# Expert phase: gathers issued ahead of adds on GpSimd, up to three adds in flight within an expert, an expert's weights loaded in four transfers

## The chip, the cores and the metric

The kernel runs on one core of a Trainium2 chip. The metric is the device time of one execution in microseconds (us). The kernel before takes 837.55 us, the median of three runs (837.42 to 838.53).

## What is computed

The kernel is one layer of a network: gated cross-attention, then a gated mixture of experts. What is counted below is mostly the second part. Cut to what matters, the reference is:

```python
x = x + tanh(g_xattn) * cross_attention(layernorm(x), ctx)     # 8 batches x 256 rows x 512 columns, 16 heads
t = layernorm(x).reshape(2048, 512)                            # 2048 tokens
probs = softmax(t @ gate_w.T)                                  # 12 experts
top_w, top_i = top_k(probs, 2);  top_w = top_w / top_w.sum()
for e in range(12):                                            # w1, w3: 320 x 512, w2: 512 x 320
    h = silu(t @ w1[e].T) * (t @ w3[e].T)
    out = out + h @ w2[e].T * cw[:, e:e + 1]                   # cw: top_w of the token where e is picked, else 0
x = x + tanh(g_ffn) * out
```

Each token has two experts, so there are 4096 pairs of token and expert, which the kernel sorts by expert.

## The kernel before

The kernel has an attention phase over eight batches and an expert phase. All matrices of the expert phase are kept as two float16 parts (a high and a low one), and each product is three matmuls. While attention runs, ScalarE (ACT) loads each expert's weights in quarters, VectorE (DVE) splits them, and ACT stores them to `w_dram` (the profile says `weight_parts`), 2 MB per expert.

**Between the phases.** SP stores the last batch's sum to `out` (L469) and its normed tokens to `xn_dram` (L474, `tokens_normed`). SP and DVE wait for that store, then the engines read a flag and branch past a second, guarded attention run (`both_runs`, L291 to L294). ACT loads the weights of experts 0 and 1 into SBUF (`W`, L670 to L676), SP those of experts 2 to 11 (L490 to L504); `W` has room for four experts (`EB`), so expert e's load waits until the last tile of expert e-4 is done, and for the load before it. Each load is one transfer of 16 KB in each of 128 partitions. DVE sorts the pairs into 43 tiles of 128 (`TILES`; a tile holds one expert's tokens, and the last tiles may be empty) and makes `slot_tok`, `slot_out`, `slot_w` (which token, which row of `out`, which weight) and `table` (which expert, as the value that the weights' semaphore must have).

**The expert phase, per tile j.** GpSimd (POOL) gathers the tile's 128 token rows to `xg[j % 4]` with an indirect DMA (L579). TensorE (PE) turns them (`turn_x`, L1274, to PSUM), DVE copies them to `xT`. PE makes both hidden products (`hidden`, L1286); ACT and DVE make silu and the product and its two parts; PE turns these (`turn_h`, L1297), DVE copies them; PE makes the down product (`down`, L1307); ACT weighs it to `yo[j % 4]` (`weigh`, L703); POOL adds it to the rows of `out` with an accumulating indirect DMA (L593). The order on PE is written out in `step` (L1312 to L1326): in step j it reads `table` twice into registers (L1279), waits for the weights, and then runs `turn_h(j-1)`, `hidden(j)`, `turn_x(j+1)`, `down(j-1)`. `tiles` (L371) peels three steps, loops over rounds of four, and peels the rest.

**The order on POOL** is the loop at L588: wait for `yo` of tile j, wait until every earlier add has landed, issue add j, then issue gather j+4 (which reuses the buffer of tile j). The adds go one after another because an accumulating DMA reads and rewrites rows of `out`, and a token of one expert may come again in another expert's tile. Within one expert no token comes twice. On ACT, `weigh` waits until add j-4 has landed, so that `yo` is free.

Of the kernel before, what the change touches and what calls it, by code (L numbers as in the profile page):

```python
# [5 lines left out]
ALU = mybir.AluOpType  # L6
# [6 lines left out]
U16 = mybir.dt.uint16  # L13

P = 128
# [19 lines left out]
def wait(eng, sem, at, k, c=0, alone=None):  # L35

    if at.i is None and k * at.add + c <= 0:  # L40
        return
    assert k * at.add + c > 0, "a wait against nothing in a loop's first round"
    value = at.value(k, c)
    if alone is not None and at.i is not None:
        value = eng.to_reg(value)
        eng.wait_ge(alone, 1)
    eng.wait_ge(sem, value)
# [45 lines left out]
def flamingo_kernel(nc, x, ctx_in, g_xattn, g_ffn, WqT, bq, WkT, bk, WvT, bv, WoT, bo, gateT, wall, out):  # L93
# [3 lines left out]
    NE = gateT.shape[1]  # L97
    WCOL = wall.shape[2]
# [7 lines left out]
    TILES = (TOP * TOK + NE * (P - 1)) // P  # L106
# [9 lines left out]
    HOT = TOP * NT // 4  # L116
    LO = 2048.0
    TR = 4
    EB = 4
    HB = 2 * (FT - 1) + 1  # L120
    assert 2 * FL == P
# [16 lines left out]
    with top:  # L138
        def sb(name, shape, dt=F32, stack=top):
            return stack.enter_context(nc.sbuf_tensor(name, shape, dt))  # L140

        def sem(name):
            return top.enter_context(nc.semaphore(name))
# [109 lines left out]
        le = sb("le", [P, TILES, NE])  # L253
        et_f = sb("et_f", [P, TILES])
        table = sb("table", [P, TILES + NE], U16)
        xg = [sb(f"xg{i}", [P, 2 * T], F16) for i in range(TR)]
        xT = [sb(f"xT{i}", [P, 2 * TT, P], F16) for i in range(2)]
        act1 = [sb(f"act1_{i}", [P, F]) for i in range(2)]
# [93 lines left out]
        s_table = sem("s_table")  # L352
# [28 lines left out]
                step(eng, At(None, 0, n), n)  # L381


        s_add = sem("s_add")
        s_stored = sem("s_stored")
        s_spare = sem("s_spare")

# [6 lines left out]
        def _(sp):  # L394
# [95 lines left out]
            for e in range(EB // 2, NE):  # L490
                if e == EB:
                    sp.wait_ge(s_table, 2)
                if e >= EB:

                    end = sp.value_load(table[0:1, TILES + e - EB:TILES + e - EB + 1], min_val=1,
                                        max_val=TILES + 1)
                    sp.wait_ge(s_y, end)
                if e == NE - 1:
                    for n in range(2):
                        sp.wait_ge(s_wst[n], 16 * 2 * NE)  # L500

                sp.wait_ge(s_wr, 16 * e)
                sp.dma_start(W[:, (e % EB) * 2 * WCOL:(e % EB + 1) * 2 * WCOL],
                             w_dram[e].rearrange("p h n -> p (h n)")).then_inc(s_wr, 16)  # L504
            sp.wait_ge(s_wr, 16 * NE)


        @block.gpsimd
        def _(pool):
# [61 lines left out]
                    .then_inc(s_tilw, 1)  # L571


            pool.wait_ge(s_tok, 1)
            def gather(j):
                if j >= TR:
# [3 lines left out]
                                        in_offset=bass.IndirectOffsetOnAxis(ap=slot_tok[:, j:j + 1], axis=0))\  # L580
                    .then_inc(s_xg[j % TR], 16)

            for j in range(TR):
                gather(j)
            pool.wait_ge(s_tok, 2)
            pool.wait_ge(s_spare, 16 * TT)
            pool.wait_ge(s_stored, 1)
            for j in range(TILES):  # L588
                pool.wait_ge(s_yo, j + 1)
                if j >= 1:  # L590

                    pool.wait_ge(s_add, 16 * j)
                pool.indirect_dma_start(out=out[:, :],  # L593
                                        out_offset=bass.IndirectOffsetOnAxis(ap=slot_out[:, j:j + 1], axis=0),
                                        in_=yo[j % TR][:, :], in_offset=None, compute_op=ALU.add)\
                    .then_inc(s_add, 16)
                if j + TR < TILES:
                    gather(j + TR)
            pool.wait_ge(s_add, 16 * TILES)


        @block.scalar
        def _(act):
# [66 lines left out]
            for e in range(EB // 2):  # L670

                if e >= 1:

                    act.wait_ge(s_wr, 16 * e)
                act.dma_start(W[:, e * 2 * WCOL:(e + 1) * 2 * WCOL], w_dram[e].rearrange("p h n -> p (h n)"))\
                    .then_inc(s_wr, 16)  # L676

            act.wait_ge(s_wexp, 1)
            act.activation(el[:, :], dl[:, :], ACT.Exp).then_inc(s_wexp, 1)
# [17 lines left out]
            def weigh(act, j, n):  # L697

                wait(act, s_y, j, 1, 2)
                if n >= TR:  # L700

                    wait(act, s_add, j, 16, 16 - 16 * TR)
                act.activation(yo[n % TR][:, :], y_ps[:, :], ACT.Copy, scale=slot_w[:, bass.ds(j.value(), 1)])\  # L703
                    .then_inc(s_yo, 1)

# [15 lines left out]
        def _(dve):  # L721
# [16 lines left out]
            def done(ins):  # L738
                steps[0] += 1
                ins.then_inc(s_r, 1)  # L740
                return steps[0]
# [284 lines left out]
            for n in range(0, PAIRS, HOT):  # L1026
# [13 lines left out]
            then(last)  # L1040
            last = done(dve.tensor_reduce(et_f[:, :], le[:, :, :], AX_X, ALU.add))
            then(last)
            last = done(dve.tensor_scalar(et_f[:, :], et_f[:, :], float(NE - 1), None, ALU.min))
            then(last)
            dve.tensor_scalar(table[:, TILES:TILES + NE], endt[:, :], 1.0, None, ALU.add).then_inc(s_table, 1)
            dve.tensor_scalar(table[:, 0:TILES], et_f[:, :], 1.0, 16.0, ALU.add, ALU.mult).then_inc(s_table, 1)

            dve.wait_ge(s_tab, 2)
            last = done(dve.tensor_scalar(slot_w[:, :], MA[:, TILES:2 * TILES], 1.0 / (LO * WS * HS), None, ALU.mult))
# [1 line left out]
            dve.scalar_tensor_tensor(out=slot_w[:, :], in0=MA[:, 0:TILES], scalar=1.0 / (WS * HS), in1=slot_w[:, :],  # L1051
                                     op0=ALU.mult, op1=ALU.add).then_inc(s_tok, 1)


            def x_out(dve, j, n):
                wait(dve, s_xt, j, 1, 1)
# [35 lines left out]
        def _(pe):  # L1092
# [183 lines left out]

            def weights_of(j):

                landed = pe.value_load(table[0:1, bass.ds(j.value(), 1)], min_val=16, max_val=16 * NE)  # L1279
                return landed, ((landed - 16) & (16 * (EB - 1))) * (2 * WCOL // 16)  # L1280

            def hidden(j, par, off):
                for n, (ps, full) in enumerate(((h1_ps, s_h1), (h3_ps, s_h))):
# [88 lines left out]
```

## Time and profile before

| | before |
|---|---|
| time, median of 3 runs | 837.55 us (837.42 to 838.53) |
| profiled execution: span, first to last instruction | 830.0 us |
| TensorE busy | 630.5 us (76%) |
| VectorE, ScalarE, GpSimd busy | 419.5, 332.3, 243.7 us |
| mean share of full clock granted to TensorE | 0.919 |
| expert phase on TensorE, first `turn_x` to last `down` | 530.4 to 817.9 us |

The span is 7.6 us shorter than the median time; the device time of the profiled execution by itself is not shown, so that difference is taken as the part around the span. All times inside the trace are in us from the first instruction. PE, PEld (its weight loads), DVE, ACT and POOL are the engines, SP issues DMAs; a q behind a name (PEldq, SPq) is the engine's sequencer, which handles registers, branches and DMA issues.

### The profile page before, as it was taken

The page shows a single profiled execution, that of the slowest core. Times are in us where ns is not written, and L with a number is a line of the kernel's source. Part 1 is how long each engine was busy: PE and PEld are TensorE (multiplying, and loading weights), DVE is VectorE, ACT ScalarE, POOL GpSimd, SP SyncE. Part 2 cuts the span into 40 slices and gives each one's busy share as a digit, 9 for nine tenths or more (in the row PEclk, how much of TensorE's full clock was granted, in tenths as well). Part 3 has the DMA queues.
Part 4 walks back from the last instruction along what each step waited for, and adds up shares of the span by engine and source line. Part 5 has one row for each costly group of instructions (what it writes and reads, how often), then busy time and mean ns, then how long its engine had stood idle before and what let it go on. Part 6 is the DMA issues. An engine that isn't in the chain of part 4 may idle for free.

```text
span 830.0 us, 13872 instructions
## 1 busy us (share of the span) xinstructions
PE 630.5 (76%) x4169; PEld 270.9 (33%) x4170; DVE 419.5 (51%) x763; ACT 332.3 (40%) x394; POOL 243.7 (29%) x186
## 2 busy tenths in 40 slices
PE   3438669888896988989767140599989898999993
PEld 1202213123131221313212010465545454666661
DVE  4777556566574766657556536553323332333330
ACT  5125656565675665656744000022222221222221
POOL 5212123151331414223012111333333333344432
PEclk9999979899999999989978555699999999999998
DMA  4677885958779495876957387155666666645452
GB/s 153 177 209 208 202 251 151 268 163 188 222 192 265 139 259 174 165 250 182 240 166 220 94 274 293 54 125 156 177 177 177 177 174 171 172 90 97 80 90 39
DMA packets 75371, 146.52 MB, mean 177 GB/s; under 512 B 10757, under 2 KB 36870, under 8 KB 73798
## 3 DMA queue, kind: packets, MB, share of 16 engines
q1 hardware_dynamic: 43664, 68.18, 30.6%
q10 hardware_dynamic: 22038, 55.35, 21.8%
q0 software_dynamic: 9632, 22.55, 14.7%
q8 instruction: 17, 0.28, 0.1%
q14 instruction: 20, 0.16, 0.1%
HBM read 87.85 MB, written 53.74 MB: 171 GB/s over the span
## 4 chain that ended last, share of the span: by engine, by line
PE 32%; DMA 29%; issue 18%; POOL 7%; DVE 7%; SPq 4%; ACT 2%; ACTq 0%; DVEq 0%; POOLq 0%
DMA out<-yo,slot_out 10%; PE S L1286 9%; DMA residual<-x 6%; PE O L1307 6%; PE O L1151 5%; PE MA L1187 4%; DMA xg<-tokens_normed,slot_tok 4%; DMA K<-k_parts 3%; PE S L1112 3%; PE MC L1187 2%; SPq L463 2%; PE S L1274 1%; DMA W<-weight_parts 1%; DMA q_parts<-qs 1%; POOL cs L536 1%
## 5 line engine op out<-in xcount | busy, mean ns | idle before, releaser
L655 ACT ACTIVATE prob<-S 128x1024 f32<-128x1024 f32 x256 | 246.1, 1023 | 183.5 <-PE S L1112 144.7
L1286 PE MATMUL S<-W,xT 128*128 x1032 | 149.1, 301 | 1.2 <-DVE xT L1060 1.2
L1151 PE MATMUL O<-prob,V 128*32 128x512 f32 x1024 | 149.3, 646 | 0.0
L1112 PE MATMUL S<-Q,K 49*128 49x512 f16 x512 | 92.5, 411 | 63.4 <-DMA K<-k_parts 41.6
L593 POOL DMA_INDIRECT out<-yo,slot_out x43 | 69.2, 1609 | 171.1 <-DMA out<-yo,slot_out 84.0
L1286 PEld LDWEIGHTS S<-W,xT 128*128 128x128 f16 x1032 | 99.3, 98 | 39.0 <-issue 1.3
L1307 PE MATMUL O<-W,hT 128*128 (+1 forms) x344 | 91.9, 387 | 0.9 <-DVE hT L1080 0.9
L1068 DVE SCALAR_TENSOR_TENSOR hh<-S,act 128x320 f32<-128x320 f32 x43 | 21.1, 492 | 123.0 <-PE S L1286 123.0
L1112 PEld LDWEIGHTS S<-Q,K 49*128 49x128 f16 x512 | 20.3, 95 | 192.7 <-ACT prob L655 134.5
L762 DVE SCALAR_TENSOR_TENSOR wp<-wf,wp 128x1024 f16<-128x1024 f32 x48 | 69.6, 1451 | 1.7
L536 POOL TENSOR_TENSOR cs<-ctx,cs 128x1024 f16<-128x1024 f32 x8 | 17.0, 2126 | 151.5 <-DVE cs L823 151.5
L703 ACT ACTIVATE yo<-O,slot_w 128x512 f32<-128x512 f32 x43 | 29.5, 687 | 78.6 <-PE O L1307 64.2
L688 ACT ACTIVATE act<-S 128x320 f32<-128x320 f32 x43 | 18.8, 437 | 88.6 <-PE S L1286 88.6
L695 ACT ACTIVATE hs<-hh 128x320 f16<-128x320 f32 x43 | 20.2, 470 | 76.5 <-DVE hh L1068 76.5
L1307 PEld LDWEIGHTS O<-W,hT 128*128 128x128 f16 (+1 forms) x344 | 32.3, 97 | 49.8 <-issue 30.7
L579 POOL DMA_INDIRECT xg<-tokens_normed,slot_tok x43 | 42.7, 993 | 18.6 <-issue 12.5
L1080 DVE COPY hT<-S 128x640 f16<-128x640 f16 x43 | 21.1, 491 | 52.1 <-PE S L1297 52.1
L760 DVE TENSOR_SCALAR wp<-wf 128x1024 f16<-128x1024 f32 x48 | 41.3, 860 | 10.6 <-DMA wf<-wall 10.5
L1187 PE MATMUL MC<-os,w4s 128*128 128x512 f16 x96 | 28.9, 442 | 18.4 <-DVE os L864 14.6
L1187 PE MATMUL MA<-cs,w4s 128*128 128x512 f16 x96 | 27.3, 416 | 19.2 <-DVE kf L875 8.4
L536 POOL TENSOR_TENSOR os<-kf,os 128x1024 f16<-128x1024 f32 x8 | 17.8, 2228 | 77.4 <-DVE os L864 77.4
L929 DVE COPY osum<-O 128x512 f32<-128x512 f32 x32 | 21.9, 683 | 35.0 <-PE O L1151 35.0
(149 smaller groups left out, 647.7 us busy)
## 6 DMA issues: line engine op xcount, KB each, us to landing
wf<-wall ACTq DMA_DIRECT2D x48, 512.0 KB, 7.0
weight_parts<-wp ACTq DMA_DIRECT2D x48, 512.0 KB, 5.0
W<-weight_parts SPq DMA_DIRECT2D x10, 2048.0 KB, 9.1
Q<-q_parts SPq DMA_DIRECT2D x48, 128.0 KB, 8.2
K<-k_parts SPq DMA_DIRECT2D x48, 128.0 KB, 8.5
ctx<-ctx_in SPq DMA_DIRECT2D x8, 512.0 KB, 12.6
residual<-x SPq DMA_DIRECT2D x8, 512.0 KB, 14.3
k_parts<-ks SPq DMA_DIRECT2D x8, 512.0 KB, 2.8
```

The lines of the kernel that those rows point to most:

```text
L536: pool.tensor_tensor(parts[:, 1], f[:, :, :], parts[:, 0], ALU.subtract).then_inc(lo, 1)
L579: pool.indirect_dma_start(out=xg[j % TR][:, :], out_offset=None, in_=xn_dram[:, :], in_offset=bass.IndirectOffsetOnAxis(ap=slot_tok[:, j:j ...
L593: pool.indirect_dma_start(out=out[:, :], out_offset=bass.IndirectOffsetOnAxis(ap=slot_out[:, j:j + 1], axis=0), in_=yo[j % TR][:, :], in_o ...
L655: act.activation(prob[:, u % RING, :], S[u % 2][:, :], ACT.Exp, scale=SCALE).then_inc(g.exp, 1)
L703: act.activation(yo[n % TR][:, :], y_ps[:, :], ACT.Copy, scale=slot_w[:, bass.ds(j.value(), 1)])\
L760: dve.tensor_scalar(wp[c % 2][:, 0], wf[c % 2][:, :], WS, None, ALU.mult).then_inc(s_whi, 1)
L762: dve.scalar_tensor_tensor(out=wp[c % 2][:, 1], in0=wf[c % 2][:, :], scalar=WS, in1=wp[c % 2][:, 0], op0=ALU.mult, op1=ALU.subtract).then_ ...
L1112: last = pe.matmul(S[u % 2][:, s * T:(s + 1) * T], K[par][r0:r0 + PARTS * DK + 1, 2 * g4 + n, st * P:(st + 1) * P], Q[par][r0:r0 + PARTS * ...
L1151: last = pe.matmul(O[g4 % 2][2 * DK * j:2 * DK * (j + 1), :], V[par][:, st, GH * g4 + j, :], prob[:, u % RING, (j % 2) * T:(j % 2 + 1) * T ...
L1187: last = pe.matmul(bank[:, :], w4s[:, wp_, w, k, m * P:(m + 1) * P], src[:, xp, k, :], start=(n == 0 and k == 0), stop=(n == len(PASSES) - ...
L1286: last = pe.matmul(ps, xT[par][:, xp * TT + k, :], W[:, bass.ds(off + (w * WCOL + (2 * k + n) * F), F)], start=(k == 0 and (xp, w) == (0, 0)),
L1307: last = pe.matmul(y_ps[:, :], hT[par][0:rows_, block, :], W[0:rows_, bass.ds(off + (w * WCOL + W2 + k * T), T)], start=(n == 0), stop=(n ...
```

## The change

On POOL, the loop runs 45 rounds (`TILES + LAG`): round j issues gather j+4 first, if there is one, and then add j-2. An add no longer waits for all earlier ones. Add j waits until add j-3 has landed, and then tells ACT so (`s_landed`); from tile 6 on it reads a small number from a new table `turns` into a register, which says whether add j must also wait for add j-1, and whether for add j-2. It must where that tile belongs to another expert, or where tile j is empty. Tiles 1 to 5 wait for the add before them as in the kernel before. Each of the four `yo` buffers has its own semaphore. `weigh` waits for `s_landed` in place of the adds' semaphore. DVE makes `turns` with six small instructions behind `slot_w`. The weights of an expert are loaded by four transfers of 4 KB per partition each, issued back to back by the same engine at the same place, and the table's values are scaled by four. `s_turns` is waited for once by POOL ahead of the loop.

```diff
@@ -116,6 +116,9 @@
     TR = 4
+    LAG = 2
+    DEEP = 3
+    PIECES = 4
     EB = 4
@@ -253,6 +256,10 @@
         table = sb("table", [P, TILES + NE], U16)
+        et_c = sb("et_c", [P, TILES])
+        turned = sb("turned", [P, 2, TILES])
+        unused = sb("unused", [P, TILES])
+        turns = sb("turns", [P, TILES], U16)
         xg = [sb(f"xg{i}", [P, 2 * T], F16) for i in range(TR)]
@@ -381,7 +388,17 @@
-        s_add = sem("s_add")
+        def load_expert(eng, e):
+            flat = w_dram[e].rearrange("p h n -> p (h n)")
+            step = 2 * WCOL // PIECES
+            for n in range(PIECES):
+                at = (e % EB) * 2 * WCOL + n * step
+                eng.dma_start(W[:, at:at + step], flat[:, n * step:(n + 1) * step]).then_inc(s_wr, 16)
+        s_add = [sem(f"s_add{i}") for i in range(TR)]
+        s_turns = sem("s_turns")
+        s_landed = sem("s_landed")
         s_stored = sem("s_stored")
@@ -499,10 +516,9 @@
-                sp.wait_ge(s_wr, 16 * e)
-                sp.dma_start(W[:, (e % EB) * 2 * WCOL:(e % EB + 1) * 2 * WCOL],
-                             w_dram[e].rearrange("p h n -> p (h n)")).then_inc(s_wr, 16)
-            sp.wait_ge(s_wr, 16 * NE)
+                sp.wait_ge(s_wr, 16 * PIECES * e)
+                load_expert(sp, e)
+            sp.wait_ge(s_wr, 16 * PIECES * NE)
@@ -571,6 +587,7 @@
+            pool.sem_inc(s_landed, TR)
             pool.wait_ge(s_tok, 1)
@@ -579,24 +596,46 @@
                     .then_inc(s_xg[j % TR], 16)
+            def add(j):
+                if j >= DEEP:
+                    pool.wait_ge(s_add[(j - DEEP) % TR], 16 * ((j - DEEP) // TR + 1))
+                    pool.sem_inc(s_landed, 1)
+                if 1 <= j < TR + DEEP - 1:
+                    pool.wait_ge(s_yo, j + 1)
+                    pool.wait_ge(s_add[(j - 1) % TR], 16 * ((j - 1) // TR + 1))
+                elif j >= 1:
+                    turn = pool.value_load(turns[0:1, j:j + 1], min_val=0, max_val=3)
+                    behind1 = pool.to_reg((turn & 1) * 16 + 16 * ((j - 1) // TR))
+                    behind2 = pool.to_reg((turn & 2) * 8 + 16 * ((j - 2) // TR))
+                    pool.wait_ge(s_yo, j + 1)
+                    pool.wait_ge(s_add[(j - 1) % TR], behind1)
+                    pool.wait_ge(s_add[(j - 2) % TR], behind2)
+                else:
+                    pool.wait_ge(s_yo, 1)
+                pool.indirect_dma_start(out=out[:, :],
+                                        out_offset=bass.IndirectOffsetOnAxis(ap=slot_out[:, j:j + 1], axis=0),
+                                        in_=yo[j % TR][:, :], in_offset=None, compute_op=ALU.add)\
+                    .then_inc(s_add[j % TR], 16)
...
             pool.wait_ge(s_stored, 1)
-            for j in range(TILES):
-                pool.wait_ge(s_yo, j + 1)
-                if j >= 1:
-                    pool.wait_ge(s_add, 16 * j)
-                pool.indirect_dma_start(out=out[:, :],
-                                        out_offset=bass.IndirectOffsetOnAxis(ap=slot_out[:, j:j + 1], axis=0),
-                                        in_=yo[j % TR][:, :], in_offset=None, compute_op=ALU.add)\
-                    .then_inc(s_add, 16)
+            pool.wait_ge(s_turns, 1)
+            for j in range(TILES + LAG):
                 if j + TR < TILES:
                     gather(j + TR)
-            pool.wait_ge(s_add, 16 * TILES)
+                if j >= LAG:
+                    add(j - LAG)
+            for n in range(TR):
+                pool.wait_ge(s_add[n], 16 * len(range(n, TILES, TR)))
@@ -671,9 +710,8 @@
-                    act.wait_ge(s_wr, 16 * e)
-                act.dma_start(W[:, e * 2 * WCOL:(e + 1) * 2 * WCOL], w_dram[e].rearrange("p h n -> p (h n)"))\
-                    .then_inc(s_wr, 16)
+                    act.wait_ge(s_wr, 16 * PIECES * e)
+                load_expert(act, e)
@@ -697,9 +735,7 @@
                 wait(act, s_y, j, 1, 2)
-                if n >= TR:
-                    wait(act, s_add, j, 16, 16 - 16 * TR)
+                wait(act, s_landed, j, 1, 1)
                 act.activation(yo[n % TR][:, :], y_ps[:, :], ACT.Copy, scale=slot_w[:, bass.ds(j.value(), 1)])\
@@ -1040,10 +1076,10 @@
             then(last)
-            last = done(dve.tensor_scalar(et_f[:, :], et_f[:, :], float(NE - 1), None, ALU.min))
+            last = done(dve.tensor_scalar(et_c[:, :], et_f[:, :], float(NE - 1), None, ALU.min))
             then(last)
             dve.tensor_scalar(table[:, TILES:TILES + NE], endt[:, :], 1.0, None, ALU.add).then_inc(s_table, 1)
-            dve.tensor_scalar(table[:, 0:TILES], et_f[:, :], 1.0, 16.0, ALU.add, ALU.mult).then_inc(s_table, 1)
+            dve.tensor_scalar(table[:, 0:TILES], et_c[:, :], 1.0, 16.0 * PIECES, ALU.add, ALU.mult).then_inc(s_table, 1)
@@ -1051,6 +1087,17 @@
+            last = done(dve.tensor_scalar(unused[:, :], et_f[:, :], NE - 0.5, None, ALU.is_gt))
+            for n in range(2):
+                last = done(dve.tensor_tensor(turned[:, n, 2:TILES], et_f[:, 2:TILES], et_f[:, 1 - n:TILES - 1 - n],
+                                              ALU.is_gt))
+            then(last)
+            for n in range(2):
+                last = done(dve.tensor_tensor(turned[:, n, 2:TILES], turned[:, n, 2:TILES], unused[:, 2:TILES], ALU.max))
+            then(last)
+            dve.scalar_tensor_tensor(out=turns[:, 2:TILES], in0=turned[:, 1, 2:TILES], scalar=2.0,
+                                     in1=turned[:, 0, 2:TILES], op0=ALU.mult, op1=ALU.add).then_inc(s_turns, 1)
@@ -1276,8 +1323,9 @@
-                landed = pe.value_load(table[0:1, bass.ds(j.value(), 1)], min_val=16, max_val=16 * NE)
-                return landed, ((landed - 16) & (16 * (EB - 1))) * (2 * WCOL // 16)
+                one = 16 * PIECES
+                landed = pe.value_load(table[0:1, bass.ds(j.value(), 1)], min_val=one, max_val=one * NE)
+                return landed, ((landed - one) & (one * (EB - 1))) * (2 * WCOL // one)
```

## Rows read from the trace of the kernel before

**Rows 1.** The page: busy time of the engines, and TensorE's clock in 40 slices.
```profile
PE 630.5 (76%) x4169; PEld 270.9 (33%) x4170; DVE 419.5 (51%) x763; ACT 332.3 (40%) x394; POOL 243.7 (29%) x186
...
PEclk9999979899999999989978555699999999999998
```

**Rows 2.** Timeline of PE: start, length, line, form, idle time before with its releaser.
```profile
539.17 0.44 PE L1297 MATMUL S<-ident,hs 128*128 128x128 f16 x5 [1.40 <-DVE hs L1075]
...
611.15 0.62 PE L1274 MATMUL S<-ident,xg 128*128 128x128 f16 x8 [2.25 <-DMA xg<-tokens_normed,slot_tok]
...
749.68 0.44 PE L1297 MATMUL S<-ident,hs 128*128 128x128 f16 x5
...
755.60 0.44 PE L1297 MATMUL S<-ident,hs 128*128 128x128 f16 x5
...
808.98 0.44 PE L1297 MATMUL S<-ident,hs 128*128 128x128 f16 x5
...
814.46 0.45 PE L1297 MATMUL S<-ident,hs 128*128 128x128 f16 x5
```

**Rows 3.** Waits, 540 to 830 us: who waited for whom, total us, times, longest.
```profile
POOL out L593 <- DMA out<-yo,slot_out: 84.0, 20, 7.4
...
PE S L1274 <- DMA xg<-tokens_normed,slot_tok: 13.6, 8, 3.4
...
PE S L1297 <- issue: 6.0, 7, 1.3
```

**Rows 4.** Timeline of POOL: adds (L593) around a weight load, then in steady state.
```profile
606.06 1.59 POOL L593 DMA_INDIRECT out<-yo,slot_out  x1 [2.63 <-DMA out<-yo,slot_out]
...
615.88 1.59 POOL L593 DMA_INDIRECT out<-yo,slot_out  x1 [6.94 <-DMA out<-yo,slot_out]
...
745.04 1.59 POOL L593 DMA_INDIRECT out<-yo,slot_out  x1 [3.04 <-ACT yo L703]
746.93 0.99 POOL L579 DMA_INDIRECT xg<-tokens_normed,slot_tok  x1 [0.30 <-issue]
750.94 1.59 POOL L593 DMA_INDIRECT out<-yo,slot_out  x1 [3.02 <-ACT yo L703]
```

**Rows 5.** Chain that ended last, in order of time: two adds, the second beside weights.
```profile
600.54 4.72 DMA out<-yo,slot_out
...
606.06 9.02 DMA out<-yo,slot_out
```

**Rows 6.** Transfers into `W`: us from issue to landing, all twelve.
```profile
DMA to landing us min/median/max: 7.7/9.1/10.8
```

**Rows 7.** Line 1279, ns: PE's reads of `table`, in 728:734 and in 617:620.
```profile
L1279 PEldq TENSOR_LOAD <-table x2: 285/621/957, 729.6 to 730.3; - x2
...
L1279 PEldq TENSOR_LOAD <-table x2: 285/559/833, 617.3 to 618.0; - x2
```

**Rows 8.** Timeline of all engines, 478 to 506 us: the first two weight transfers.
```profile
486.22 9.48 ACTq L675 DMA_DIRECT2D W<-weight_parts  x2
```

**Rows 9.** Chain that ended last, between the two phases.
```profile
488.51 8.09 DMA tokens_normed<-xs
...
497.59 5.99 issue
```

**Rows 10.** Line 293, ns: PE's branch past the second attention run.
```profile
L293 PEldq COMPARE_BRANCH  x1: 3622/3622/3622, 494.6 to 494.6; - x1
```

**Rows 11.** Line 474: the same store one batch earlier.
```profile
DMA to landing us min/median/max: 3.3/3.3/3.3
```

**Rows 12.** Timeline of all engines: DVE ahead of its first copy, and two late adds.
```profile
529.00 0.20 DVE L1051 SCALAR_TENSOR_TENSOR slot_w<-MA,slot_w 128x43 f32<-128x43 f32 x1
...
531.07 0.69 DVE L1060 COPY xT<-S 128x1024 f16<-128x1024 f16 x1 [1.87 <-PE S L1274]
...
815.61 1.55 POOL L593 DMA_INDIRECT out<-yo,slot_out  x1 [3.90 <-ACT yo L703]
...
821.00 1.55 POOL L593 DMA_INDIRECT out<-yo,slot_out  x1 [3.84 <-DMA out<-yo,slot_out]
```

## The prediction

> **What bounds the kernel now.** I read the page first. TensorE is the busiest engine with 630.5 us, but its share of the span is 76%, and its clock digits show nines with dips where it had nothing to do [rows 1]. So the question is where it waits, not how fast it multiplies. The change touches the expert phase and the transfers just ahead of it, so I went to the timeline of PE there. One line is good for counting tiles: `turn_h` (L1297) runs once a tile. In the steady stretch two of them start at 749.68 and 755.60, 5.92 us apart, at full clock and with PE never idle [rows 2]. From the first start (539.17) to the last (814.46) are 42 steps and 275.3 us. Had all run steadily, they would take 41 x 5.92 plus the last one, which has no `turn_x`, 5.48 (808.98 to 814.46): 248.2 us. **PE loses 27.1 us in this phase**, all of it before 737.
>
> The waits say to whom. PE waits 13.6 us for gathers, and 6.0 us, seven times, for "issue" just ahead of `turn_h`; POOL meanwhile waits 84.0 us for its own adds [rows 3]. The row at 611.15 is one of the late gathers, 2.25 us [rows 2]. The rest of the 27.1 is one down product at half clock after such a wait, and `turn_h` and `turn_x` starting some tenths late.
>
> The timeline of POOL tells why gathers are late. Gather j+4 stands behind add j, and add j behind the landing of add j-1. An add usually lands in 4.72 us, but beside a weight load it takes 9.02 [rows 5], so POOL's next add starts 9.8 us after it (606.06 to 615.88) [rows 4]. SP starts such a load when an expert's last tile is done, which is when that tile's add starts. The adds of an expert of three tiles then take 9.8 + 2 x 5.5 = 20.8 us (an undisturbed add, 4.72, and 0.8 to the next issue make 5.5), while PE needs 3 x 5.92 = 17.8. The chain of adds is the bound by 3.0 us an expert. Eight experts' ends start such a load, and 8 x 3.0 = 24 us is about what PE loses. Behind the last load, adds follow PE in 5.9 us (745.04 to 750.94) [rows 4] and nothing is lost.
>
> **Part 1: gathers ahead, several adds in flight.** Nothing is removed from POOL; the order changes. Gather j+4 now needs only `turn_x(j)` and the add three places back to have been issued, so it starts about four steps (23.7 us) ahead of its use. Before, it had about two. Its landing, 4 to 9 us, is covered by that. The adds: of three tiles of an expert, the first must wait for the last of the expert before (9.8 us after it, as now); the second and third wait for adds that have landed by then, so POOL's own work spaces them. That is 1.59 for the add, 0.99 for the gather, 0.3 and 0.8 of issue between them [rows 4], and the new register read. PE's reads of the same kind take 0.285 us, up to 0.957 [rows 7]; with a few register operations I take 0.5. That makes 4.2 us a tile, 3.7 to 5.2 by the bounds, against 5.92. An expert's adds now take 9.8 + 2 x 4.2 = 18.2 us at the old landing time, 0.4 over PE's 17.8, and less by Part 2. Over eight experts that lag is 3.2 us at most, and POOL may be 5 us late before anyone waits: in the worst place `weigh` of tile j needs POOL to be at add j-1, and with an add of 9.0 us POOL is there about 5.3 us early.
>
> What goes is therefore the whole 27.1, if the 6.0 of "issue" go with the late gathers. I looked at what that is. Before each tile PE's sequencer reads `table` twice; normally 0.285 us each, but a read that falls on the start of an add's data takes up to 0.9. At 728 to 734, after a slightly late gather, the stretched read leaves PE idle; at 617 to 620, with the gather in time, a read of 833 ns costs nothing, because the sequencer is ahead of the array [rows 7]. All seven gaps follow a late gather. I leave 1 us of the 27.1 (bounds 0 and 9: the 6.0 stay, and 3 of new small waits). **Gain 26 us.**
>
> **Part 2: four transfers a load.** In the expert phase it shortens the adds beside a load: they share the DMA engines with pieces of a quarter of the size. Between 4.72 and 9.02 [rows 5] I take 6.5; an expert's adds then take 7.3 + 8.4 = 15.7 us, under 17.8. It gains nothing more there, but makes Part 1 safe. The load itself takes 9.1 us, at most 10.8 [rows 6], and is used three experts later; three more issues of 0.34 us on SP have nobody behind them.
>
> Ahead of the phase it may pay. The store of the last normed tokens is issued at 488.51, 2.3 us after the first weight load (486.22) [rows 8], and lands after 8.09 us on the chain [rows 9]; one batch earlier, with no weight load, it took 3.3 [rows 11]. If it can slip in after a quarter of the load, it gains 0 to 4.8 us; as it must still share, I take 2. Then DVE branches past the second attention run and stands for 5.99 us [rows 9], beside the second load; PE's own branch took 3.62 [rows 10]. The difference, 2.4, is the bound; I take 2. **Gain 4 us, bounds 0 and 7.** I reason that a DMA engine serves the other queue only after the load's share. The Trainium skill says the mechanism more exactly (DMA: Bandwidth & Descriptors, Queues, rings and completion order): an engine goes round its queues by whole packets of many descriptors. By that rule a store would wait for one quarter in place of all, and these 4 us would be near 5; the row of 8.09 against 3.3 agrees but does not prove it.
>
> A rule of the same page speaks against the change (Bandwidth): batch transfers to 1 MiB or more. Its fit for a single transfer (Anatomy of one DMA) has 2.0 us fixed; if each quarter paid it, a load would take 6 us longer, an estimate of 15.1. That is still under an expert's 17.8 us, but two of three adds would lie beside it; it raises the chance of rival B by a few hundredths.
>
> **Costs hidden elsewhere.** DVE's six new instructions of about 0.2 us, some waiting for the one before, take 1.2 us at most. DVE is done with `slot_w` at 529.20 and stands 1.87 us until `xT` at 531.07 [rows 12], where it waits for PE and the first gather; without that cover they would cost 1.2. POOL has its first gathers in hand until later than that, so its wait for `turns` is nothing. The tail stays: the last adds start at 815.61 and 821.00 [rows 12], 5.4 apart, the second waiting for the first; 43 tiles is the most there can be, and eight experts used 25, so the last are empty, and an empty tile waits as before. Where the last is not empty, 2 us more are won.
>
> **Sum.** The span is 830.0 and the median 837.55; I make the sum against the profiled span and carry the 7.6 around it over unchanged. 830.0 - 26 - 4 = 800.0, and with the rest 807.6. I say **807.6 us**.
>
> **The rivals.**
> - *A, the forecast, 807.6* (0.70). Own range 803.4 (27.1 and 7 gained) to 819.5 (18 and 0).
> - *B, the wait moves.* Adds beside loads do not shorten but grow, and POOL is behind at each expert change until `weigh` waits. It needs an add over 14 us beside a load; 9.02 speaks against it, adds that now overlap each other speak for it. Half of the 27.1 stays: 837.6 - 13.5 - 2 = 822 us (0.11).
> - *C, reads collide at every step.* A gather is now issued just behind `turn_x`, when PE's sequencer reads `table`. If gathers stretch the read as an add's start does, by up to 0.67, and half of the steps show 0.5 to 1: about 20 us come back, 828 us (0.07). Against it: the stretched reads of before lie about 2 us behind the add, not by the gather.
> - *D, slower: POOL becomes the bound.* PE's mean step is 275.3 / 42 = 6.56 us. If POOL's round of gather, read, waits and add takes more than that, the kernel is slower; I count 4.2, so the read and its arithmetic would have to take 2.9 in place of 0.5. At 7.0 us a round: 42 x 1.08 = 45 in place of 27, and 837.6 + 18 - 4 = 852 us (0.06).
> - *E, it does not do what it says.* If `turns` made nearly every add wait, the chain of adds would stay at 7.3 + 2 x 5.5 = 18.3 (or 20.8) an expert, and only gathers' lead and buffers would help: half of the gain, 820 us (0.06).
>
> **How the numbers follow.** The range takes A's own, and reaches to B and E for most of their weight: 803.5 to 822.5. About 0.2% (1.7 us) is what a measurement of this kernel tells from no change. Only D is slower, and a part of C could be: slower 0.07, within 0.2% 0.02, faster 0.91.
>
> **What would show it.** PE's `turn_h` starts 5.92 us apart from the second step on, with no wait of L1274 for `xg` and no "issue" ahead of L1297 over 0.3 us. POOL's first add of an expert starts up to 3 us late, the others with `yo`. Adds beside loads land in 6 to 7 us. The store of L474 lands in about 6 us, and DVE stands 4 us behind its branch. The prediction is wrong if `weigh` waits for POOL, if POOL's round exceeds 5.92 us, or if reads at L1279 cost PE time without a late gather.

## The result, and the profile of the changed kernel

The changed kernel takes 804.74 us, the median of four runs (801.29 to 809.25), against 837.93 us before (837.42 to 838.53, four runs on the same chip). The ratio is 0.9636, with a 95% interval of 0.9576 to 0.9696. The profiled execution took 808.14 us with a span of 806.4, so 1.7 us lie around the span.

From the page of the changed kernel, busy times and TensorE's clock, to be read against [rows 1]:

```profile
PE 624.7 (77%) x4169; PEld 270.1 (33%) x4170; DVE 420.2 (52%) x769; ACT 332.5 (41%) x394; POOL 243.1 (30%) x186
...
PEclk9859979999999998999998855579999999999997
```

The clock digits show nines all through the phase in both kernels, before and after. What has gone is too short for a digit. In the trace of the kernel before, PE was busy for 1.7 of the 4 us from 692 to 696, and then the granted clock stood at half (1.2 of 2.4 GHz) until 699.5. The down product in that stretch took 3.69 us, where one at full clock takes 2.10:

```profile
696.17 3.69 PE L1307 MATMUL O<-W,hT 128*128 x8
```

In the changed kernel the granted clock is full from the first `turn_h` to the last. The timeline of PE in the changed kernel, `turn_h` now at L1345, answers to [rows 2]:

```profile
541.60 0.44 PE L1345 MATMUL S<-ident,hs 128*128 128x128 f16 x5 [1.40 <-DVE hs L1122]
...
547.57 0.44 PE L1345 MATMUL S<-ident,hs 128*128 128x128 f16 x5
...
553.49 0.44 PE L1345 MATMUL S<-ident,hs 128*128 128x128 f16 x5
...
559.41 0.44 PE L1345 MATMUL S<-ident,hs 128*128 128x128 f16 x5
...
789.94 0.45 PE L1345 MATMUL S<-ident,hs 128*128 128x128 f16 x5
```

From 541.60 to 789.94 are 248.3 us, where the kernel before took 275.3. After the first step (5.97) every step is 5.92 us. PE loses 0.1 us in the phase; it lost 27.1. The waits of POOL in the changed kernel, 540 to 807 us, answer to [rows 3] (adds at L620, gathers at L596):

```profile
POOL out L620 <- DMA out<-yo,slot_out: 61.1, 11, 7.1
POOL out L620 <- ACT yo L739: 50.6, 23, 8.0
POOL xg L596 <- PE S L1321: 38.3, 21, 6.1
```

Gathers now wait for PE, not PE for gathers. POOL still waits for adds, but 11 times in place of 20. Its timeline around a weight load answers to [rows 4]:

```profile
595.62 1.59 POOL L620 DMA_INDIRECT out<-yo,slot_out  x1 [7.08 <-DMA out<-yo,slot_out]
597.51 0.99 POOL L596 DMA_INDIRECT xg<-tokens_normed,slot_tok  x1 [0.30 <-issue]
598.80 1.59 POOL L620 DMA_INDIRECT out<-yo,slot_out  x1 [0.30 <-issue]
600.70 0.99 POOL L596 DMA_INDIRECT xg<-tokens_normed,slot_tok  x1 [0.30 <-issue]
602.12 1.59 POOL L620 DMA_INDIRECT out<-yo,slot_out  x1 [0.44 <-ACT yo L739]
```

The add at 595.62 opens an expert and waited for the one before it. The next follows 3.2 us later, with a gather between them, and the third as soon as `yo` is there.

The chain that ended last, between the phases, answers to [rows 9]:

```profile
490.69 7.75 DMA tokens_normed<-xs
...
499.44 5.40 issue
```

Here little has changed: 8.09 and 5.99 us before.

Two things must be told apart in all that follows. An execution's time moves by some us either way, and the traces show where: the last store of normed tokens was issued anywhere from 482.6 to 495.8 us in the traces of this study, because the attention phase ran shorter or longer. So I compare stretches of a trace that leave attention out: **the phase**, from the first `turn_h` to the last (248.2 us without a loss), and **the way to it**, from the issue of that store to the first `turn_h` (539.17 - 488.51 = 50.7 us before, 541.60 - 490.69 = 50.9 in the changed kernel).

### The profile page after: what moved, and what is told of

Same layout as the page of the kernel before. It is cut to its first block, busy times and chain, and to the rows that moved or that the text cites. A ratio compares the mean times of both kernels' runs of the same rounds, so it can differ in the third digit from the quotient of the medians.

```text
span 806.4 us, 14236 instructions
## 1 busy us (share of the span) xinstructions
PE 624.7 (77%) x4169; PEld 270.1 (33%) x4170; DVE 420.2 (52%) x769; ACT 332.5 (41%) x394; POOL 243.1 (30%) x186
## 4 chain that ended last, share of the span: by engine, by line
PE 42%; issue 22%; DMA 16%; DVE 10%; POOL 6%; SPq 2%; ACT 1%; POOLq 0%; DVEq 0%; ACTq 0%
PE S L1334 15%; PE O L1355 9%; PE O L1198 5%; DMA residual<-x 4%; PE MA L1234 4%; DMA out<-yo,slot_out 4%; PE MC L1234 2%; PE S L1159 2%; PE S L1321 2%; DMA inverse_sums<-zr 1%; POOL cs L552 1%; DMA K<-k_parts 1%; PE S L1345 1%; POOL xs L576 1%; DMA wf<-wall 1%
## 5 line engine op out<-in xcount | busy, mean ns | idle before, releaser
L620 POOL DMA_INDIRECT out<-yo,slot_out x43 | 68.6, 1596 | 114.5 <-DMA out<-yo,slot_out 61.1
L596 POOL DMA_INDIRECT xg<-tokens_normed,slot_tok x43 | 42.6, 992 | 50.5 <-PE S L1321 38.3
L1234 PE MATMUL MA<-cs,w4s 128*128 128x512 f16 x96 | 29.9, 445 | 20.4 <-DVE kf L911 9.3
L552 POOL TENSOR_TENSOR os<-kf,os 128x1024 f16<-128x1024 f32 x8 | 17.8, 2226 | 79.9 <-DVE os L900 79.9
L1234 PE MATMUL MC<-os,w4s 128*128 128x512 f16 x96 | 27.6, 426 | 18.0 <-DVE os L900 14.2
```

The costliest lines, as they stand in the source:

```text
L552: pool.tensor_tensor(parts[:, 1], f[:, :, :], parts[:, 0], ALU.subtract).then_inc(lo, 1)
L596: pool.indirect_dma_start(out=xg[j % TR][:, :], out_offset=None, in_=xn_dram[:, :], in_offset=bass.IndirectOffsetOnAxis(ap=slot_tok[:, j:j ...
L620: pool.indirect_dma_start(out=out[:, :], out_offset=bass.IndirectOffsetOnAxis(ap=slot_out[:, j:j + 1], axis=0), in_=yo[j % TR][:, :], in_o ...
L1234: last = pe.matmul(bank[:, :], w4s[:, wp_, w, k, m * P:(m + 1) * P], src[:, xp, k, :], start=(n == 0 and k == 0), stop=(n == len(PASSES) - ...
```

## Experiments

Times are medians; each ratio is to the kernel before on the same chip, with its 95% interval.

**The kernel before, twice more.** No edit.

> The kernel before, once more, for a second profile. The timed gain (33 us) is larger than the 23.6 us between the two profiled spans. Theory: the phase loses 27 us here too, and the rest is the start of the phase, which moves by some us from execution to execution (the last store was issued between 484.4 and 495.8 us in nine traces). Rival: the phase itself loses more in most executions, 30 to 33 us, and the first profile was a lucky one.

> The same again, for a third profile: the same two theories, 27 us lost in the phase or 30 to 33.

The two executions took 826.05 and 833.71 us; the phase lost 26.8 and 30.6 us, the way to it took 50.9 and 51.8. The third one's costliest step, from its PE timeline, 640 to 670 us:

```profile
645.42 3.43 PE L1286 MATMUL S<-W,xT 128*128 x24
654.29 1.04 PE L1274 MATMUL S<-ident,xg 128*128 128x128 f16 x8 [5.43 <-DMA xg<-tokens_normed,slot_tok]
655.11 3.31 PE L1307 MATMUL O<-W,hT 128*128 x8
```

That step takes 13.15 us, and the granted clock is 0.57 from 654 to 658. This trace has three such stretches near half clock in the phase (562 to 565.5, 654 to 657.5, 698.5 to 702), each behind a late gather; the other two have one each. Of the 30.6 us, PE stands idle for 21.4, against 20.4 in both other traces, and is busy for 2.5 and 2.8 us longer than in them. So the extra loss is for the most part time at the lower clock, not waiting.

The loss is 27 us twice and 31 once. Neither theory is settled for the timed runs: the profiled executions of this kernel (826.05, 833.71, and 831.7 by the first one's span) were at the short end of its timed ones (829.89 to 844.23), and one was under all of them.

**The changed kernel again.**

> The changed kernel once more, on the chip of the other three. Theory: PE loses nothing in the phase (248.3 us from the first turn_h to the last), 50 to 51 us from the last store's issue to the first turn_h, and what differs from run to run lies in the attention phase. Rival: the no-loss phase was one lucky execution, and gaps of 1 to 10 us show here.

803.25 us, ratio 0.9596 (0.9548 to 0.9644). The phase took 248.5, the way to it 50.9 (484.5 to 535.4). The first theory holds; the empty phase was no luck.

**One transfer a load.** The changed kernel with

```diff
-    PIECES = 4
+    PIECES = 1
```

> The changed kernel with each expert's weights in one transfer again. Theory (the 27 us come from the order on GpSimd alone, and the trace of the changed kernel shows only 0.9 us won ahead of the phase): PE's turn_h (5 transposes a tile) still starts every 5.92 us, 248.3 us from first to last, and the time is that of the changed kernel within 1 to 2 us. Rival 1 (my forecast's second part): 4 us slower than the changed kernel, because the store of the normed tokens and DVE's branch stand behind a whole load. Rival 2: adds beside a load take longer than the 10.2 us they take now, GpSimd falls behind, and PE's steps show gaps again.

807.62 us, ratio 0.9668 (0.9621 to 0.9716). The phase lost 0.4 us, the way took 51.0 (484.4 to 535.4). By the traces the changes on GpSimd alone, gathers ahead and adds in flight, bring the 27 us. Adds beside a load took 10.7 us (the median of the 15 that took over 7), against 9.6 in the changed kernel (of 10), and it costs nothing. In time it is within 3 to 4 us of the changed kernel, and executions of one kernel differ by more than that, so rival 1's 4 us are not excluded by the times. The way to the phase shows 0.1 between these two traces; what all twelve traces show of it stands under Part 2 below.

**The four transfers alone.** `load_expert` with four pieces in the kernel before, and the semaphore's values times four.

> The kernel before with only the four transfers. Theory: adds beside a load are not shorter than 9 us, the chain of adds still binds, PE loses 25 to 30 us in the phase and the time is that of before within 2 us. Rival (the forecast's term of 6.5 us for such an add): the adds of a three-tile expert take 18.3 us in place of 20.8, most of the stall goes, and the kernel is 15 to 20 us faster than before.

835.19 us, ratio 0.9981 (0.9933 to 1.0029). The phase lost 27.6 us. From its waits, 540 to 834 us (adds at L601):

```profile
POOL out L601 <- DMA out<-yo,slot_out: 97.1, 23, 7.4
```

Adds over 7 us took 8.8 us at the median, as in the kernel before. The rival falls: a load in four pieces does not let an add through sooner.

**Adds one after another, gathers ahead.** The changed kernel with

```diff
-                if 1 <= j < TR + DEEP - 1:
+                if j >= 1:
```

> The changed kernel, but every add waits for the one before it to land, as before; gathers still go ahead, four transfers. Theory (the chain of adds was the bound): three adds take 11.0 + 2 x 5.8 = 22.6 us against PE's 17.8, GpSimd falls behind by 4.8 us an expert, the four yo buffers absorb 5 to 12 us once, and PE loses 15 to 30 us again, now through weigh. Rival (gathers standing behind adds were the whole cause): PE loses nothing, 248 us, and the time is that of the changed kernel.

829.5 us, ratio 0.991 (0.9858 to 0.9962). No gather is late any more; in its waits PE now stands for `yo`, and ACT for POOL (530 to 800 us for PE, to 830 for ACT):

```profile
PE O L1355 <- ACT yo L739: 8.2, 4, 2.6
...
ACT yo L739 <- POOLq L605: 57.7, 17, 6.7
```

The stall takes this form, on PE's timeline:

```profile
661.47 2.11 PE L1355 MATMUL O<-W,hT 128*128 x8 [2.58 <-ACT yo L739]
```

The first 17 steps are without a loss, then the buffers are full and each of four experts costs 2.5 to 4.1 us: 13.8 in the phase, with 3.5 us at half clock among them (704.5 to 708). Another 6.8 come behind it, where POOL works off its backlog: 23.1 us from the last `turn_h` to the end against 15.5 to 16.6 elsewhere. The chain of adds was a bound by itself, and it is the theory's 15 to 30 (20.6). From 562 us to the end nearly every add starts about 0.8 us after the one before it has landed, so the chain sets the sum of the two. How it is split depends on `weigh`, which in this kernel waits until POOL has come to add j-1; in the kernel before it waited for the landing of add j-4. The profiled execution was the fastest of its six (820.57).

**Adds in flight, gathers behind them.** One transfer a load, and

```diff
-            for j in range(TILES + LAG):
+            for j in range(TILES):
+                add(j)
                 if j + TR < TILES:
                     gather(j + TR)
-                if j >= LAG:
-                    add(j - LAG)
```

> The changed kernel's rule for the adds (up to three in flight within an expert), but each gather issued behind the add of its round as before, and one transfer a load. Theory (the chain of adds was the bound): an add that opens an expert is up to 4 us late and the gather behind it too, which uses up its spare lead; PE loses 0 to 10 us of the 27. Rival (the place of the gathers was the cause): PE loses 20 us or more.

823.7 us, ratio 0.9865 (0.9817 to 0.9912). The phase lost 17.6 us, between the two theories, and both were too simple. The waits of PE, 540 to 830 us, and a late pair on POOL:

```profile
PE S L1319 <- DMA xg<-tokens_normed,slot_tok: 6.7, 8, 2.1
PE S L1343 <- issue: 3.1, 4, 1.2
```

```profile
566.41 1.58 POOL L620 DMA_INDIRECT out<-yo,slot_out  x1 [2.96 <-DMA out<-yo,slot_out]
568.30 0.98 POOL L596 DMA_INDIRECT xg<-tokens_normed,slot_tok  x1 [0.30 <-issue]
577.03 1.59 POOL L620 DMA_INDIRECT out<-yo,slot_out  x1 [7.75 <-DMA out<-yo,slot_out]
```

Tiles 1 to 5 still add one after another, and the gather behind an add beside a load lands after 8.5 us; the costliest step, 9.8 us, lies there. That step also holds 3.5 us at half clock (576.6 to 580.1), right behind a late gather. By the traces, freeing the adds alone brings 9.5 of the 27.1, moving the gathers alone 6.5 (27.1 - 20.6), both together 27.0. The medians on that chip say much the same: 12.0, 6.2 and, with one transfer, 28.1 us.

**The gather one round ahead.** One transfer a load, and

```diff
-    LAG = 2
+    LAG = 1
```

> The changed kernel with one transfer a load and the gather only one round ahead: gather j+4 stands behind add j-2 in place of add j-3 (behind add j it lost 17.6 us). Theory: one round, 5.9 us, is more than the 0.1 to 3.9 us by which gathers came late there, so PE loses 0 to 1 us. Rival (a first add of an expert that waits for the last one still holds the gather too long): 3 us or more.

802.93 us, ratio 0.9635 (0.9574 to 0.9695). The phase lost 0.3 us and PE waited for no gather. The theory holds: one round is enough, and the change's second one is spare. This run and the one with the gathers behind differ only in where the gather stands, so its place alone is worth the 17.4 us between them once adds are in flight.

**More work on GpSimd.** A memset ahead of each add, of 1024 or of 2048 columns. It stands in for a dearer round:

```diff
+                pool.memset(idle[:, :], 0.0).then_inc(s_idle, 1)
```

(Two more lines make it wait for the memset before it.)

> The changed kernel with a memset of 1024 columns (about 0.9 us) ahead of every add on GpSimd. Its round in a backlog is 3.2 us now, with this 4.1. Rival, the forecast's own threshold (a round may take up to PE's 5.92 us): no loss, 248.3 us. Theory (the first add of an expert starts 11 us after the last of the expert before, so two rounds more must fit into 17.8 - 11 = 6.8 us, and the threshold is 3.4): an expert's adds take 19.2 us, GpSimd falls behind 1.4 us an expert and 11 us over eight; the buffers hide most of it, and PE loses 0 to 5 us.

> The same with 2048 columns (about 1.8 us), so a round of 5.1 us. Rival, the forecast's threshold: still under 5.92, no loss. Theory: an expert's adds take 11 + 2 x 5.1 = 21.2 us against 17.8, 3.4 us behind an expert, 27 over eight; less 8 to 12 us of buffers, PE loses 12 to 20 us.

805.54 us, ratio 0.9631 (0.9582 to 0.9679), and 802.99 us, ratio 0.9593 (0.9542 to 0.9645). The phase lost 0.3 and 0.4 us. My new theory of a threshold at 3.4 us falls, and the timeline of POOL in the second one shows why:

```profile
599.37 1.82 POOL L606 MEMSET idle<- 128x2048 f32 x1
601.36 1.59 POOL L625 DMA_INDIRECT out<-yo,slot_out  x1 [0.17 <-issue]
603.26 0.98 POOL L598 DMA_INDIRECT xg<-tokens_normed,slot_tok  x1 [0.30 <-issue]
604.24 1.83 POOL L606 MEMSET idle<- 128x2048 f32 x1
609.07 1.59 POOL L625 DMA_INDIRECT out<-yo,slot_out  x1 [3.00 <-DMA out<-yo,slot_out]
```

SP had issued the weights at 597.18; the last add of the expert came 4.2 us later and landed in 6.9 us, not in 11. The first of the next followed 7.7 us behind it, and 7.7 + 2 x 4.9 is 17.5, under PE's 17.8. For six of the eight experts the last add landed in 6.5 to 7.2 us, for the other two in 8.4 and 9.1. The reading that fits is that a late add meets less of the load, so the chain rights itself; no run varies that alone. Rounds of 4.9 us cost nothing, as the forecast's own threshold has it. Where the threshold lies was not reached.

**The first loads behind the branches.** The changed kernel with (shortened)

```diff
-            for e in range(EB // 2):
-                if e >= 1:
-                    act.wait_ge(s_wr, 16 * PIECES * e)
-                load_expert(act, e)
+            act.wait_ge(s_done, 2)
+            load_expert(act, 0)
             act.wait_ge(s_wexp, 1)
...
+            act.wait_ge(s_wr, 16 * PIECES)
+            load_expert(act, 1)
```

SP also holds expert 3's load back until the first gathers have been used.

> The changed kernel, but the loads of experts 0 and 1 start only when PE and DVE are past their branches, and expert 3's when the first gathers have been used. Theory (the first loads delay the store of the normed tokens and DVE's branch, and four transfers did not help since the store still came last): the store lands in 3.3 to 4.5 us in place of 7.8, DVE stands 3 to 4 us behind its branch in place of 5.5, and from the issue of that store to the first turn_h it takes 44 to 47 us in place of 50.9; 4 to 6 us faster than the changed kernel. Rival (the store waits for the store of the sum ahead of it in its own queue, and the branch for the code itself): no change, 50 us.

801.62 us, ratio 0.9594 (0.9551 to 0.9638). The store of the tokens, first here and then in the changed kernel:

```profile
DMA to landing us min/median/max: 3.2/3.2/3.2
```

```profile
DMA to landing us min/median/max: 7.8/7.8/7.8
```

So the first weight load was what held the store, by 4.6 us. DVE's next instruction starts 3.9 us behind its branch in place of 5.4, and it is now released by PE, whose own branch takes 3.94. But the way to the phase shrank only from 50.9 to 47.7 (490.95 to 538.68). ACT's timeline has the rest:

```profile
500.96 3.26 ACTq L397 DMA_DIRECT2D W<-weight_parts  x4
504.27 0.22 ACT L714 ACTIVATE el<-dl 128x16 f32<-128x16 f32 x1 [49.23 <-issue]
```

Issuing four transfers holds ACT for 3.26 us, and DVE waits for `el` behind them.

**The same with one transfer.** `PIECES = 1`.

> The changed kernel with the first loads behind the branches and one transfer a load, so without the four transfers. Theory: with the loads out of the way of the store and the branches the four transfers are worth nothing; 47 to 49 us from the last store's issue to the first turn_h, no loss in the phase, the time of the same kernel with four transfers (801.6) within 2 us. Rival (smaller transfers help the gathers and adds beside them): 2 us or more slower, with gaps in PE's steps.

801.25 us, ratio 0.9606 (0.9566 to 0.9647). The phase lost 0.1 us. ACT's timeline now:

```profile
492.80 0.34 ACTq L397 DMA_DIRECT2D W<-weight_parts  x1
493.64 0.21 ACT L714 ACTIVATE el<-dl 128x16 f32<-128x16 f32 x1 [46.42 <-DVE dl L980]
```

The way takes 45.4 us (482.8 to 528.2), 5.5 less than in the changed kernel and 2.3 less than with four transfers, better than I expected of it. By its trace it is the fastest version, and it does without the four transfers. Its median is 2 to 3.5 us under the changed kernel's two, which the intervals do not separate.

## Why the prediction held, and where it did not

The forecast was 807.6 us, the measured median 804.74, and the kernel went the way of case A. By its steps:

- **The bound (right).** 27.1 us lost for adds and gathers beside weight loads. Both halves of the argument carry: with adds serial 20.6 us come back, with gathers behind 17.6. The forecast counted one down product at half clock. That holds for the trace it was read from; another of the same kernel has three such stretches, and the one of the four transfers alone has none and lost 27.6 us all the same.
- **Part 1, 26 us (right).** 27.0 in the two profiles. The 1 us left for gaps was not needed. The reading of the seven "issue" gaps holds: from the changed kernel, PE's reads of `table`, 555 to 560 us,

```profile
L1327 PEldq TENSOR_LOAD <-table x2: 287/612/937, 556.9 to 558.3; - x2
```

  one read of 937 ns, and the next `turn_h` at 559.41, on time. Stretched reads cost PE nothing without a late gather. In the kernel before [rows 7] they did.
- **POOL's round, 4.2 us (too high).** Backlogged rounds take 3.2 (595.62 to 598.80). The gap ahead of the add is 0.30 us, where the forecast put 0.8 and 0.5 for the register read. That the sequencer does waits, read and arithmetic while the gather is being made is the reading that fits; no run isolates it.
- **An add beside a load, 6.5 us (wrong).** The add that is issued as a load starts takes 9.2 to 11.4 in the changed kernel, longer than the 9.02 of [rows 5], and the four transfers alone leave it at 8.8. The step that failed is "they share the DMA engines with pieces of a quarter of the size". It did no harm: 10.4 + 0.8 + 2 x 3.2 = 17.6 us is just under 17.8, as the shorter round made up for the longer add, and the longest one, 11.37, made the next expert open 18.6 us after the one before at no cost. By the forecast's own count the margin was gone there; that the chain has more was seen only in the run with the memset.
- **Part 2, 4 us (wrong).** 0.3 + 0.6 us between the two profiles, and -0.2 over the whole way, which includes 1.1 us more in the first `hidden` as the clock rose later. One pair of traces says little here. Of the twelve with the first loads in their old place, six have one transfer a load and six have four (they differ in their adds and gathers too, but these come later). The store landed in 7.7 to 8.3 and in 7.7 to 8.6 us: nothing gained. DVE stood behind its branch for 5.9 to 6.2 and for 4.1 to 6.2 us, 6.0 and 5.0 in the mean, so about 1 of the 2 us was there, though not in every execution. The way took 50.9 and 50.3 us in the mean. The mechanism was half right: the first load does hold the store. What failed is "it can slip in after a quarter of the load". In the changed kernel the store was issued at 490.69; from 491 to 495 us the DMA queues held

```profile
q10 hardware_dynamic: 324, 1.17, 98.6%
```

  and nothing else, and from 495.5 to 498

```profile
q1 hardware_dynamic: 523, 0.52, 58.9%
q10 hardware_dynamic: 83, 0.27, 27.0%
```

  q10 is ACT's queue with the weights, q1 SP's with the store. The store still came last. The Trainium skill's rule in DMA: Bandwidth & Descriptors (Queues, rings and completion order), that an engine goes round its queues packet by packet, would have let it in sooner as the forecast read it; the measurement decides, and why the four transfers stay together is open.
- **The price of four transfers (open in the forecast, small).** The Trainium skill's rule in DMA: Bandwidth & Descriptors (Bandwidth), of 1 MiB or more a transfer, does not show in the first load: its last piece landed 8.7 us after the first was issued (488.3 to 497.0), and one transfer before took 9.1. In the phase it does: the four pieces took 11.9 to 13.7 us from first issue to last landing in the changed kernel, one transfer 9.1 to 11.6 in the run with one; about 1.4 us of the difference is the later issue of the last piece. The forecast's 15.1 was not reached; the 2.0 us behind it is a fit that the Trainium skill gives (Anatomy of one DMA) for transfers issued from GpSimd, and these came from SP and ACT.
- **DVE's six instructions (right).** They end at 531.36 in the changed kernel, ahead of the first copy's wait:

```profile
531.16 0.20 DVE L1099 SCALAR_TENSOR_TENSOR turns<-turned 128x41 uint16<-128x41 f32 x1
532.43 0.69 DVE L1107 COPY xT<-S 128x1024 f16<-128x1024 f16 x1 [1.06 <-PE S L1321]
```

- **The tail (0.9 us off).** 16.5 us from the last `turn_h` to the end, 15.5 before. The new waits ahead of the last adds may take some of it; that was not looked into.
- **The sum's base (wrong).** The 7.6 us around the span was no such thing. It is 1.7; the profile shown of before was of a short execution, of about 831.7 us. By profiles the gain is 23.6 us (830.0 to 806.4: 27.0, less 2.4 for a later start and 0.9 in the tail, to rounding), by timed medians 33.2. With 1.7 for the base and nothing for Part 2 the sum would have been 830.0 - 26 + 1.7 = 805.7. The 5.9 us too much and the 4 that did not come hid most of each other, which was luck. Some 6 us of the timed gain (33.2 less the phase's 27.0) are in no trace here. The third profile of the kernel before, with 30.6 lost, may be a part of it; that is argued, not shown. Nor can 1.7 us be told from no change in four to six executions: the intervals above reach about 3.5 to 5 us to either side.

The rivals B, C and E did not come about; in the changed kernel's waits `weigh` waited for PE alone, all 43 times. For D, rounds up to 4.9 us were tried and cost nothing.

## What to carry to other kernels

Where one in-order engine issues both what must wait (accumulating transfers) and what must only be early (gathers), put the early ones a round ahead, and relax the waits to what the data demand: each alone brought a quarter to a third of the gain, both all of it. An engine that stands for a few us can lose more than that behind the wait: look at the granted clock of the stretch too. Look at the issuing engine before cutting a transfer up: here the pieces let neither an add nor the store through sooner, took longer to land in the phase, and in the version with late first loads held ScalarE for 3.3 us with something urgent behind them. And sum against the same execution's time as its span, or against two or three profiles, when executions differ by more than the terms.

## What was not expected of the hardware

- A 2 MB load issued 2.3 us ahead of a 512 KB store on another queue delays its landing from 3.2 to between 7.7 and 8.6 us, in one transfer or in four.
- PE's branch past the second attention run took 3.9 and 3.7 us with the DMA queues free (the two kernels with late first loads), and DVE, which then waits for PE, went on 3.9 and 3.8 us behind its own. Beside the loads PE's took 3.4 to 4.1 us, while DVE, which branches last, stood for 5.9 to 6.2 behind loads of one transfer and 4.1 to 6.2 behind loads of four. What decides within that range is open.
- An accumulating transfer beside a load took 8.8 us at the median one at a time, 9.6 to 10.7 with others in flight (up to 12.75), and 6.9 when it started 4.2 us into the load. With the smaller memset it took 8.8 (the median of the eight over 7 us) although others were in flight, so overlap alone does not decide it.
- After PE has stood for a late gather (2.2 to 5.4 us) TensorE's granted clock can fall to half for about 3.5 us: once in the phase of two traces of the kernel before, three times in the third, never with the four transfers alone, and never in the eight traces in which PE had no such wait.
